# The two short attentions of a transformer kernel, worked in passes of two heads and half the queries

## The reference, cut to what matters

```python
# self0, 1024 tokens, H = 16 heads, dk = 8
scores = jnp.einsum('bhqd,bhkd->bhqk', q, k) / np.sqrt(dk)
attn = jax.nn.softmax(scores, axis=-1)
o = jnp.einsum('bhqk,bhkd->bhqd', attn, v)
# self1, the same with a causal mask
mask = jnp.tril(jnp.ones((S, T), dtype=bool))
scores = jnp.where(mask, scores, -jnp.inf)
```

## Time and profile before

| | us |
|---|---|
| median of three runs (lowest, highest) | 2885.43 (2884.71, 2887.26) |
| the profiled execution | 2884.41 |
| its span, first to last instruction | 2882.7 |
| cross0, pass B | about 133 to 1104 |
| self0, first to last exponential | 1186.5 to 1399.5 |
| self1, first to last exponential | 1517.5 to 1674.7 |

### The profile page before, as it was taken

How to read it: one execution, slowest core, us unless ns; L and a number is a source line. 1 busy time by engine, 2 the same in 40 slices (tenths; PEclk the granted TensorE clock), 3 DMA queues, 4 the chain that set the end, 5 groups by cost and what they waited for, 6 DMA issues and landing times.

```text
span 2882.7 us, 57521 instructions
## 1 busy us (share of the span) xinstructions
PE 2455.8 (85%) x22475; PEld 777.0 (27%) x22475; DVE 2370.1 (82%) x2782; ACT 2154.9 (75%) x4063; POOL 226.4 (8%) x556
## 2 busy tenths in 40 slices
PE   3499999999999994799459955999999999999955
PEld 2222222222222221222123312222222222222223
DVE  6699999999999983677337635999999999999824
ACT  3189999999999994466315641899999999999941
POOL 4001101010000001000000040000000010000000
PEclk8699999999999997899769966999999999999987
DMA  4211111101101100110111132011101111011000
GB/s 136 71 33 40 41 43 43 41 28 35 34 28 40 29 5 18 49 35 29 36 50 37 39 103 68 26 30 31 38 28 38 31 29 40 28 36 33 6 4 8
DMA packets 76606, 109.17 MB, mean 38 GB/s; under 512 B 17600, under 2 KB 56308, under 8 KB 76340
## 3 DMA queue, kind: packets, MB, share of 16 engines
q1 hardware_dynamic: 74548, 101.12, 12.0%
q0 software_dynamic: 1792, 4.37, 0.8%
HBM read 73.93 MB, written 22.42 MB: 33 GB/s over the span
## 4 chain that ended last, share of the span: by engine, by line
PE 67%; DVE 18%; ACT 6%; issue 4%; SPq 2%; DMA 2%; POOL 1%; ACTq 0%; POOLq 0%; DVEq 0%
PE ps L1280 66%; DVE maxima L1094 12%; ACT probs L884 3%; ACT probs L846 2%; DVE scratch L960 1%; SPq L448 1%; DVE maxima L1053 1%; ACT acc_out L827 1%; POOL probs L648 1%; DMA qa_stage<-q_cross 1%; DMA o_self<-acc_out 0%; PE ps L1288 0%; DVE stats L965 0%; DVE z L975 0%; DVE z L960 0%
## 5 line engine op out<-in xcount | busy, mean ns | idle before, releaser
L1094 DVE TENSOR_REDUCE maxima<-ps 128x1 f32<-128x920 f32 x1792 | 1889.9, 1111 | 102.0 <-PE ps L1280 102.0
L884 ACT ACTIVATE probs<-ps 128x512 f32<-128x512 f32 (+1 forms) x3264 | 1762.4, 594 | 146.3 <-PE ps L1280 146.1
L1280 PE MATMUL ps<-probs,v_stage 128*16 128x256 f32 (+1 forms) x13568 | 1150.0, 403 | 1.5 <-ACT probs L846 1.1
L1280 PE MATMUL ps<-k_stages,qa_stage 64*128 64x460 bf16 (+2 forms) x4032 | 801.5, 370 | 182.9 <-DMA qa_stage<-q_cross 67.3
L1280 PE MATMUL ps<-qb_stage,k_stages 64*128 64x512 bf16 (+4 forms) x3712 | 799.0, 381 | 42.3 <-ACT probs L846 17.6
L1280 PEld LDWEIGHTS ps<-k_stages,qa_stage 64*128 64x128 bf16 (+1 forms) x4032 | 209.5, 94 | 1023.8 <-issue 507.8
L1280 PEld LDWEIGHTS ps<-probs,v_stage 128*16 128x16 f32 x13568 | 234.8, 94 | 422.0 <-issue 364.5
L1053 DVE TENSOR_REDUCE maxima<-ps 128x1 f32<-128x1024 f32 (+7 forms) x256 | 246.8, 987 | 111.6 <-PE ps L1280 110.3
L846 ACT ACTIVATE probs<-ps 128x512 f32<-128x512 f32 (+1 forms) x448 | 229.4, 556 | 141.8 <-PE ps L1280 136.9
L1280 PEld LDWEIGHTS ps<-qb_stage,k_stages 64*128 64x128 bf16 (+1 forms) x3712 | 208.1, 93 | 343.6 <-ACT probs L846 99.9
L654 POOL COPY v_stage<-by_key 128x400 f32<-128x400 f32 (+1 forms) x96 | 40.5, 423 | 1376.0 <-PE ps L1280 1211.4
(11 more groups left out here) (212 smaller groups left out, 932.7 us busy)
## 6 DMA issues: line engine op xcount, KB each, us to landing
k_stages<-k_cross SPq DMA_DIRECT2D x64, 150.2 KB
k_stages<-k_cross SPq DMA_DIRECT2D x64, 150.0 KB
k_cross<-probs SPq DMA_DIRECT2D x24, 384.0 KB, 2.7
scratch<-acc_out SPq DMA_DIRECT2D x512, 16.0 KB
k_stages<-k_cross SPq DMA_DIRECT2D x64, 100.1 KB
k_stages<-k_cross SPq DMA_DIRECT2D x64, 100.0 KB
qa_stage<-q_cross SPq DMA_DIRECT2D x128, 48.0 KB
qb_stage<-q_cross SPq DMA_DIRECT2D x128, 48.0 KB, 4.8
```

The source lines that it names most:

```text
L884: return nc.scalar.activation(probs[0:m, probs_slot(a, j, i), :], ps[0:m, b_bank(a, use), :], ACT.Exp, scale=float(E) ** -0.5)
L1094: nc.vector.tensor_reduce(maxima[:, at, seg:seg + 1], ps[:, A_BANK + 2 * (g % 2):A_BANK + 2 * (g % 2) + 2, 0:a.segment], AX_XY, ALU.max).t ...
L1280: return nc.tensor.matmul(out_, lhsT, rhs, start=start, stop=stop)
```

## The change

`self_plan` becomes `short_plan`, and `attention` becomes `short_attention` on each engine. A pass is a pair of heads, one on partitions 0 to 63 and one on 64 to 127, and half of the queries; there are 16 passes in each attention. A step is one tile of 128 keys for both heads, so two tiles of pass B. A full pass has 8 steps; in self1 the first half of the queries has 4.

- Pass A's unit is 128 queries by up to 512 keys, two matmuls of 64 rows, one for each head. VectorE reduces both in one instruction to two maxima.
- VectorE only joins the maxima. GpSimd splits them in four small linked operations. ScalarE copies the turned rows, after step 3 (in a first half of self1 after step 0). The turned rows share three banks with pass B.
- Values lag by three steps (`lag`), in halves of 256 columns, the last batch of a pass at once. ScalarE copies the accumulators out at step 2.
- Pass A runs two passes ahead, in self1 four units further (`extra`).
- The masks of the diagonal are still matmuls of 128 rows, now one for each head.
- SyncE stages a pair of heads by eight DMAs: three of keys and one of queries for each head, the latter writing `qa_stage` and `qb_stage` at once (`q_stages`). The maxima of a pass go in two DMAs. `put_maxima` now stands ahead of `store_out`.
- `clear_mask_row` and its eight DMAs go; GpSimd clears both query stages after cross0 (`clear_queries`).

The diff, cut to its core:

```diff
-def self_plan(name, keys, causal, ring, lead, b_banks, p_slots):
+def short_plan(name, keys, causal):
...
+    a.ring, a.sides, a.p_slots, a.b_banks = 4, 2, 16, 3
...
+    a.passes = [(pair, half) for pair in range(H // 2) for half in range(HALVES)]
...
+    a.lag = 3
+    a.copy_step = a.lag - 1
+    a.extra = 4 if causal else 0
+    a.turn_step = [0 if causal and half == 0 else 3 for _, half in a.passes]
...
+        def pair_goal(a, j, t):
+
+            n = len(a.steps[j])
+            units = len(a.units[j + 2]) if j + 2 < a.n else 0
+            goal = a.units_before[min(j + 2, a.n)] + a.extra + ceil_div((t + 1) * units, n)
+            return min(a.units_before[a.n], goal, a.units_before[2] + a.extra // 2 + 2 * (a.steps_before[j] + t))
...
+                        sp.dma_start(q_stages[base:base + ROW_MAX, :, slot, :],
+                                     a.q_dram[h].unsqueeze(1).to_broadcast([ROW_MAX, 2, N])).then_inc(done, DMA)
...
+                for j in range(a.n):
+                    pair, half = a.passes[j]
+                    if half == 0 and pair >= 1 and pair + a.ring - 1 < H // 2:
+
+                        sp.wait_ge(sem(a.name + "_scores"),
+                                   pair_tile_use(a, j - 1, len(a.steps[j - 1]) - 1, a.sides - 1) + 1)
+                        stage(pair + a.ring - 1)
+                    if j + 1 < a.n:
+                        put_maxima(j + 1)
+                    if j >= 1:
+                        store_out(j - 1)
...
+                for step, (j, t) in enumerate(a.all_steps):
+                    values_step(step - a.lag)
+                    goal = max(given, pair_goal(a, j, t))
+                    for g in range(given, goal):
+                        pass_a(g)
+                    given = goal
+                    pass_b(j, t)
+                    if t == a.turn_step[j] and j + 1 < a.n:
+                        turn_maxima(j + 1)
```

More of the change, by code:

```diff
@@ L111, in self_plan @@
-    a.turn_at = 3
-    a.turn_unit = a.max_at.index(next(at for at in a.max_at if at >= a.turn_at))
-    a.ring_uses = len(a.max_units)
+    a.stage_dmas = 4 * a.sides
+    a.passes = [(pair, half) for pair in range(H // 2) for half in range(HALVES)]
+    a.n = len(a.passes)
+    a.stagings = H // 2
+    qts = NT // HALVES
+    half_units = [[(qt, c, min(BANK, last - c)) for qt in range(half * qts, (half + 1) * qts)
+                   for last in [(qt + 1) * P if causal else keys] for c in range(0, last, BANK)]
+                  for half in range(HALVES)]
@@ new lines, in short_plan, with before @@
+    half_steps = [[(kt, 0 if kt < 2 else max(0, kt * P - half * BANK) if causal else 0) for kt in range(a.key_tiles)
+                   if not causal or kt * P < (half + 1) * BANK] for half in range(HALVES)]
+    a.units = [half_units[half] for _, half in a.passes]
+    a.steps = [half_steps[half] for _, half in a.passes]
+    a.all_units = [(j, u) for j in range(a.n) for u in range(len(a.units[j]))]
+    a.all_steps = [(j, t) for j in range(a.n) for t in range(len(a.steps[j]))]
+    def before(counts):
+        return list(itertools.accumulate(counts, initial=0))
@@ L339, in transformer @@
             a.q_dram = dram("q_" + a.name, [H, TERMS * E, N], BF16)
-            a.staged_before = sum((b.n if b.cross else H) // b.ring * b.stage_dmas for b in before)
+            a.staged_before = sum(b.stagings // b.ring * b.stage_dmas for b in before)
             if not a.cross:
```

493 lines of the change are left out of this document (243 added, 250 removed).

## The result

The changed kernel takes **2822.54 us** (median of 4 runs, 2819.92 to 2825.03) beside 2885.07 of the kernel before (2883.87 to 2887.26), a ratio of 0.9782 with a 95% interval from 0.9765 to 0.9799. The forecast was 2825, and the range 2794 to 2856 holds the result. Its profiled execution took 2820.49 us, span 2818.9, which is 63.8 less than the span before.

The account below looks back on a forecast made before the run. VectorE was taken to bound cross0, TensorE and waits between engines self0, TensorE self1. Profiled 2884.4 - 49 (self0) - 12 (self1) = 2823.4, the median 1.0 above: 2825 us forecast, range 2794 to 2856.

Parts of the forecast that it names:

- The mechanism of self0: self0: ScalarE becomes the longest engine at 9.6 us a pass; self0 takes 164 us instead of 213, -49.
- the loss: self0: three engines so close lose 7% to each other over the 9.6 floor, giving 10.3 us a pass.
- The ranking of what is behind ScalarE: self0, a pass: ScalarE 9.6 us, then VectorE 9.3, then TensorE 8.9.
- SyncE in self0: self0: maxima landed 8.6 us after a pair's staging starts, needed some 11 us later, so hidden.
- A pair of 16.2: self1: TensorE's sum of 14.4 us for a pair of heads, plus 12% lost to waits, makes 16.2 us.
- Waits of 3.1 at four pairs: self1, pairs 1 to 4: second half's maxima stand behind the staging, landed at 8.6 us, needed at 5.5.
- Up to 0.7 in the other four: self1, pairs without staging: the maxima's path exceeds a first half's four steps, up to 0.7 us of waiting each.
- The start, +4: self1's start: 32 staging DMAs stand ahead of the first maxima, which go in two DMAs: +4 us.
- The masks' price: self1: each change of tile shape to or from a mask costs 0.10 us; the masks' changes 25 us in all.
- full drain: Rival, self1: each change to or from a mask costs 0.27 us, 42 us more, total 2867; chance 0.09.
- Closer packing: Rival: engines lose next to nothing, self1's maxima land in time: self0 155, self1 130, total 2800; chance 0.11.
- The clock rival: Rival: after self1's waits for maxima the clock stays at 1.2 GHz, self1 some 235 us, total 2914; chance 0.03.

Follow-up runs that it names:

- rows, outputs, staging: SyncE's loop issues the maxima row, then outputs, then a pair's staging, against the changed kernel's staging, maxima, outputs: 2812.45 us, ratio 0.975.
- the first experiment: SyncE's loop issues the next maxima row ahead of a pair's staging, outputs still last, against the changed kernel: 2865.99 us, 43 us slower.

## Why the prediction was right, and where it was not

The time came within 3 us of the forecast, and in part by luck: self0 gained 7 us more than said, and self1 with its start 5 us less. The mechanism of self0 held, self1's terms held in kind, and these were mis-sized.

**self0: the floor, not the loss.** The term was 10.3 a pass, from a floor of 9.6 and a loss of 7% that no row showed. Measured: 9.65, the floor. The mechanism held: ScalarE's sum is the pass (fewer maxima change nothing, shorter exponentials shorten it). The mis-sized term is the loss. It was chosen between cross0's 2% and the 19% of self0 before, which had two banks. Fourteen intervals take 135.5 us instead of 144.2, and the first and last passes 21.2 instead of 20.2, so the stage came 7.7 below 164.4. The ranking of what is behind ScalarE failed too: VectorE's 9.3 was put second and TensorE's 8.9 third. TensorE's work was right (8.95), but its wait at the pass's edge makes it 9.31.

**Where the gain comes from.** The prediction took three banks into its loss as something that lessens it, and put the gain on the half-array matmuls. With two banks the half-array matmuls bring 0.5 us a pass at the full clock (12.99 against 13.47), and with the clock's falls nothing: self0 217.5 against 212.5 before. Whether the third bank alone, without the half-array matmuls, would have given the gain isn't known: no run has it.

**SyncE in self0** was hidden, as said, but with an argument that missed its order. The term counted staging + rows + landing against the need for the rows. It never counted the outputs, which stand last in the queue and on whose landing the next copy waits: in the changed kernel the last issue ends at 1218.72, with 2.5 of landing, as in self1's chain, that is 1221.2, and the next copy is at 1221.46. So an estimated 0.2 us were left (one copy of the fifteen did wait, 0.4 us), and one transposition in the loop cost 43 us.

**self1: right sum, wrong parts.** Predicted 126.9 + 15 + 4 = 146 in its stage; measured 144.8, with 5.8 at the start that lie outside this stretch. With its start self1 gained 6.6 us, not 12, and self0's 7 us of surplus made it good. By term:
- A pair of 16.2: measured 16.95 to 16.97. TensorE's busy time in it is 15.5 to 15.7, not 14.4, and the loss behind it 8 to 9% instead of 12%. The mis-sized piece is mostly the values: ten pieces were put at 3.9, but each takes 0.56 to the next matmul (1561.12 to 1561.68) with 0.10 of it the change, as the earlier trace rows have it too, so 4.6. The two turns of a pair, in the old order's count with 0.5, were left out of the new sum; by their starts they take 0.14. Some 0.3 us stay open.
- Waits of 3.1 at four pairs, 12.4: measured 9.3 to 9.4 (the four staged pairs are 1.5 to 2.9 longer than 16.95), and they vanish when the staging goes last. Right place and cause, a quarter too large, though the 9.3 hold some 1.2 us of the lower clock behind two of the waits (estimated: 7.83 and 7.63 between two copies, less 5.15 without a wait and the waits of 1.84 and 2.08).
- Up to 0.7 in the other four: nothing of rows of maxima, but 0.3 a pair of the accumulator copy, which was not named.
- The start, +4: 5.8 measured, with another cause. The 32 staging DMAs ended with the row's own path. It was the first pair's staging (+2.8, its eight DMAs and their landing) and what lies between the first maxima and the first exponential (+3.0), where VectorE works off the seven units of pass A that TensorE has ahead of the first pass B.

**Outside both attentions** nothing was predicted, and +3.4 came from the clock in the mixture of experts and -5.1 behind self1, whose cause wasn't looked for.

**The masks' price** was the term taken from the nearest row, 0.10, against 0.27 for a full drain. Measured 0.10 to 0.11 at the masks. Leaving out all 32 masks of a pair takes 3.2 us of TensorE's busy time and 1.7 to 2.1 of the pair. The Trainium skill's rule in "TensorEngine Tiling (Array Packing)", section "Tiling Modes", that changing the mode drains the array, isn't contradicted: if this is the drain, it costs 0.10 us.

**The other rivals.** Closer packing (2800) was half true: self0 came at 156.7 where it had 155, self1 didn't, and reached 130 only when SyncE's order, the copy and the masks were changed; then the kernel takes 2807. The clock rival had the right place and the wrong size: behind two of the four waits, of 1.84 and 2.08 us idle, the granted clock was 0.50 in 1517.5 to 1520.5 and in 1538.5 to 1541, and back at 1.00 after each, which cost an estimated 1.2 us, where the rival said 89. Without the waits (rows, outputs, staging) it stayed at 1.00 from 1481 to 1600. In the first experiment the mechanism is large: behind a wait of 5.44 us a pair of matmuls took 0.61 instead of 0.38, and a waiting pass's stretch had 0.76. The Trainium skill's "TensorE: Matmul & The Clock Gate", section "Why this matters for your kernels", names idle gaps between bursts as what lowers the clock; the first experiment agrees with it (0.76), and so do two of the changed kernel's four waits (0.50).

## What to carry to other kernels

Where a queue waits for one transfer, what stands ahead of the wait is free as long as it ends before the awaited data are there (in self0 it did, in self1 it was 2.4 us too long), and what stands behind it is late: count every transfer of the loop against its own reader, outputs into a single buffer too. When a tile comes in two halves, give its ring a place more than the halves need; here the packing gained next to nothing without it. An experiment that shortens one engine's work to the value that theory has for the next engine doesn't show which engine is next; shorten that one as well.

## What was not expected of the hardware

- Work of ScalarE and TensorE interleaved within 0.02 us of each other (two exponentials 1.09, a step of TensorE 1.09 to 1.10) loses nothing over eight steps: 9.65 us against a sum of 9.6.
- The landing of a small output DMA behind its last issue took 2.5 us here (1573.68), against 1.98 in the earlier trace rows, and sets the least distance of two copies at 5.14 us with one buffer.
- The DMA that writes one head's queries to two places takes 0.32 to 0.34 us of SyncE's time, no more than one of those that wrote a single copy (0.34 and 0.41).
- In self1 waits of TensorE of 1.84 and 2.08 us were each followed by a stretch with a granted clock of 0.50, two others (1.92 and 1.58 us) were not.
